# Two transformer layers on one core: FP4 input groups in two pieces, late key rounding at the slot's end, constant products placed anew

## What is computed

```python
h = _layernorm(x) * (1 + ca) + sa
x = x + ga * attention(h)              # layer 0: RoPE; one position beyond the causal mask
h = _layernorm(x) * (1 + cb) + sb
x = x + gb * ffn(h)                    # layer 0: FP4; layer 1: mixture of 8 experts, top 2, and a shared one

def fp4_quant_dequant(x):              # blocks of 16 along the last dimension
    scale = max(abs(block)) / 6
    idx = searchsorted(_MID, abs(block / scale))
    return _GRID[idx] * sign * scale
h = silu(fp4_linear(x, w_gate)) * fp4_linear(x, w_up)      # 352 wide
out = fp4_linear(h, w_down)
```

## Time and profile before

| | us |
|---|---|
| three runs, median | 727.2 |
| lowest, highest | 727.04, 727.38 |
| the profiled execution | 725.66 |
| its span, first to last instruction | 723.9 |
| TensorE busy, share | 640.5, 88% |
| VectorE busy, share | 473.1, 65% |
| ScalarE busy, share | 341.8, 47% |
| GpSimd busy, share | 225.4, 31% |
| mean granted clock of TensorE, of full | 0.974 |

### The profile page before, as it was taken

One profiled execution on the slowest core, in us unless ns is written; L12 is line 12 of the kernel. 1 busy time (PEld: TensorE's weight loads), 2 busy tenths in 40 slices (PEclk: granted clock), 3 DMA queues, 4 the chain that ended last, 5 costly groups with the idle time before them and its releaser, 6 DMA issues.

```text
span 723.9 us, 10992 instructions
## 1 busy us (share of the span) xinstructions
PE 640.5 (88%) x3840; PEld 497.7 (69%) x3858; DVE 473.1 (65%) x1258; ACT 341.8 (47%) x705; POOL 225.4 (31%) x247
## 2 busy tenths in 40 slices
PE   5788899998878989988899998968889997899996
PEld 4356687877656778774668786846678885576774
DVE  5956499675767557726569776586744436766665
ACT  1133454565535464543445465443555552554553
POOL 3325545453544211004555445264410002000000
PEclk9979999999989999999999999998999999999999
DMA  8400000000000000000000000000000000001001
GB/s 261 117 1 1 1 2 1 1 2 0 1 1 1 0 1 1 1 1 1 1 0 2 0 1 1 1 1 1 1 1 1 2 2 0 1 15 30 15 24 34
DMA packets 12077, 9.64 MB, mean 13 GB/s; under 512 B 1708, under 2 KB 10744, under 8 KB 12024
## 3 DMA queue, kind: packets, MB, share of 16 engines
q1 hardware_dynamic: 12024, 8.94, 4.2%
HBM read 6.84 MB, written 2.10 MB: 12 GB/s over the span
## 4 chain that ended last, share of the span: by engine, by line
PE 65%; DVE 16%; ACT 8%; POOL 7%; issue 4%; DMA 1%; SPq 0%; POOLq 0%; ACTq 0%; DVEq 0%
PE ps L787 14%; PE ps L657 12%; PE ps L765 8%; PE ps L936 4%; PE ps L938 4%; PE ps L937 4%; PE ps L616 4%; PE ps L810 2%; PE ps L675 2%; PE ps L811 2%; PE ps L826 2%; ACT xn L1053 2%; DVE xn L1339 1%; PE ps L838 1%; DVE xn L1258 1%
## 5 line engine op out<-in xcount | busy, mean ns | idle before, releaser
L1113 ACT ACTIVATE probsT<-ps 128x512 f32<-128x512 f32 (+3 forms) x160 | 85.3, 533 | 172.1 <-PE ps L765 172.1
L787 PE MATMUL ps<-v_sb,probsT 128*128 128x129 f32 (+1 forms) x1148 | 157.1, 280 | 3.7 <-ACT probsT L1115 3.7
L787 PEld LDWEIGHTS ps<-v_sb,probsT 128*128 128x128 f32 (+1 forms) x1148 | 141.5, 191 | 10.7 <-ACT probsT L1115 5.6
L1376 DVE TENSOR_REDUCE row_max<-ps 128x1 f32<-128x512 f32 (+2 forms) x144 | 88.2, 620 | 61.3 <-PE ps L657 26.3
L765 PE MATMUL ps<-ident,probs 128*128 128x128 f32 (+1 forms) x574 | 92.6, 278 | 14.6 <-ACT hT L1043 7.8
L1087 ACT ACTIVATE probs<-ps,neg_max 128x512 f32<-128x512 f32 (+7 forms) x158 | 92.7, 617 | 15.8 <-DVE neg_max L1383 12.0
L765 PEld LDWEIGHTS ps<-ident,probs 128*128 128x128 f32 (+1 forms) x574 | 65.4, 139 | 45.6 <-issue 41.8
L515 POOL TENSOR_TENSOR hq<-ha,hp 128x352 f32<-128x352 f32 x32 | 29.9, 933 | 128.7 <-DVE hp L1419 128.7
L657 PE MATMUL ps<-k_high,q_high 128*128 128x512 f32 (+4 forms) x110 | 44.9, 408 | 2.3 <-ACT probs L1087 2.2
L1188 ACT ACTIVATE probs<-ps 128x512 f32<-128x512 f32 x40 | 24.0, 599 | 44.8 <-PE ps L938 44.8
L1391 DVE RECIPROCAL rsum<-ps 128x1 f32<-128x1 f32 x64 | 10.5, 165 | 50.3 <-PE ps L787 50.1
(11 more groups left out here) (243 smaller groups left out, 1376.7 us busy)
## 6 DMA issues: line engine op xcount, KB each, us to landing
out<-x_sb SPq DMA_DIRECT2D x8, 256.0 KB, 2.3
x_sb<-in_L_attn_x SPq DMA_DIRECT2D x2, 512.0 KB, 5.5
hT_all<-in_L_wmod SPq DMA_DIRECT2D x2, 384.0 KB
rope_cos<-table_cos SPq DMA_DIRECT2D x1, 768.0 KB, 6.8
rope_sin<-table_sin SPq DMA_DIRECT2D x1, 768.0 KB, 8.3
rope_cos<-table_cos SPq DMA_DIRECT2D x1, 256.0 KB, 3.6
rope_sin<-table_sin SPq DMA_DIRECT2D x1, 256.0 KB, 4.9
moe_raw<-in_L_ffn_expert_gate_w SPq DMA_DIRECT2D x1, 256.0 KB, 3.9
```

The lines of the kernel that those rows point to most:

```text
L787: mm = pe.matmul(bank(OUT_AT, 0, V_W), probsT[0:size, n % 4, k * P:(k + 1) * P], v_sb[0:size, j, :], start=(c == 0 and k == 0), stop=(c == ...
L1113: ins = act.activation(probsT[:, n % 4, 0:full], bank(TURN, 0, full), ACT.Copy)
L1376: ins = dve.tensor_reduce(dst, ps[:, start:start + width], AX.X, ALU.max, negate=single)
```

## The change

- The FP4 input group is rounded by GpSimd and turned by TensorE in two pieces: tile 0 (key fp4_first) at slot 6 + 4g, tiles 1 to 3 (fp4_rest) at slot 7 + 4g. gate_up waits for the first with its tile 0 and for the rest with its tile 1. ScalarE copies the two pieces apart.
- ScalarE's normalise_1 signals each tile, and modulate_1 is eight instructions of 128 columns instead of two of 512. VectorE still waits for all four tiles.
- From slot 4 on, round_rope (ScalarE) stands at the slot's end, and rope_low (GpSimd) behind hq_scaled. This concerns Q2 in slot 4, K3 in slot 5 and Q3 in slot 6.
- Constant products: none at slot 6; 2, 8, 10 and 5 before the turns of norm2 groups 0 to 3 (slots 13, 17, 21, 25), after the wait for the bank and before that for the input; 11 in batch 0 and 18 in batch 1 before the last norm3 group instead of 9, and 4 behind it; 10 in the mixture of experts before the wait for the totals.

The diff, cut to its core:

```diff
+FP4_PARTS = ((0, 1), (1, GROUP))
-WAITS_AT_HEAD = {FFN_LAG: 11, TILES + 1: 8, TILES + 5: 10}
+WAITED_FOR = {("norm2", 0): 2, ("norm2", 1): 8, ("norm2", 2): 10, ("norm2", 3): 5}
...
-    firsts = (("fp4_in", FFN_LAG), ("norm2", DOWN_LAG + GROUP + 1), ("norm3", TILES + GROUP + 2))
+    firsts = (("fp4_first", FFN_LAG), ("fp4_rest", FFN_LAG + 1), ("norm2", DOWN_LAG + GROUP + 1), ("norm3", TILES + GROUP + 2))
...
                 def modulate_1(g):
-                    h = xn[:, g, :].rearrange("p (t d) -> p t d", d=P)
-                    row = lambda k: mod_row_now[:, k, :].unsqueeze(1).to_broadcast([P, GROUP, P])
-                    pool.wait_ge(xn1_ready, b * GROUPS + g + 1)
-                    pool.tensor_tensor(h, h, row(1), ALU.mult).then_inc(h_step, 1)
-                    pool.wait_ge(h_step, b * 2 * GROUPS + 2 * g + 1)
-                    pool.tensor_tensor(h, h, row(0), ALU.add).then_inc(h_step, 1)
+                    tiles = [xn[:, g, t * P:(t + 1) * P] for t in range(GROUP)]
+                    first = b * TILES + g * GROUP
+                    def add_shift(t):
+                        pool.wait_ge(h_scaled, first + t + 1)
+                        pool.tensor_tensor(tiles[t], tiles[t], mod_row_now[:, 0, :], ALU.add).then_inc(h_shifted, 1)
+                    for t in range(GROUP):
+                        pool.wait_ge(xn1_ready, first + t + 1)
+                        pool.tensor_tensor(tiles[t], tiles[t], mod_row_now[:, 1, :], ALU.mult).then_inc(h_scaled, 1)
+                        if t:
+                            add_shift(t - 1)
+                    add_shift(GROUP - 1)
...
                 def xq_scaled(g):
-                        pool.wait_ge(turned, TURN_AT[b, "fp4_in", g - 1] + 1)
-                    pool.tensor_tensor(xq[:], qa[:], qp[:], ALU.add).then_inc(xq_step, 1)
...
+                        pool.wait_ge(turned, TURN_AT[b, "fp4_rest", g - 1] + 1)
+                    for part, (a, z) in enumerate(FP4_PARTS):
+                        cols, done = slice(a * P, z * P), b * 4 * GROUPS + 4 * g + 2 * part
+                        pool.tensor_tensor(xq[:, cols], qa[:, cols], qp[:, cols], ALU.add).then_inc(xq_step, 1)
+                        pool.wait_ge(xq_step, done + 1)
+                        pool.tensor_tensor(xq[:, cols], xq[:, cols], qp[:, cols], ALU.subtract).then_inc(xq_step, 1)
...
                 for s in range(SLOTS):
-                    if early_group(s, K0_SLOT + 1) is not None:
-                        rope_low(early_group(s, K0_SLOT + 1), 0)
-                    if early_group(s, Q0_SLOT + 1) is not None:
-                        rope_low(early_group(s, Q0_SLOT + 1), 1)
+                    if s < FP4_SLOT:
+                        rope_lows(s)
...
                         hq_scaled(s - FFN_LAG)
+                    if s >= FP4_SLOT:
+                        rope_lows(s)
...
                 def turn_group(key):
-                    if kind == "fp4_in":
-                        pe.wait_ge(xq_ready, b * GROUPS + g + 1)
+                    if kind in ("fp4_first", "fp4_rest"):
+                        part = int(kind == "fp4_rest")
+                        pe.wait_ge(xq_ready, 2 * (b * GROUPS + g) + part + 1)
                         bank_free(key)
-                        for t in range(GROUP):
+                        for t in range(*FP4_PARTS[part]):
...
+                    bank_free(key)
+                    keep_clock(TURN, WAITED_FOR.get(key, 0))
...
-                    bank_free(key)
                     turn_normed(g)
...
                 def gate_up(n):
-                    if t == 0:
-                        out_of_bank(("fp4_in", g))
+                    if t < 2:
+                        out_of_bank((("fp4_first", "fp4_rest")[t], g))
...
-                    if s in WAITS_AT_HEAD:
-                        keep_clock(3, WAITS_AT_HEAD[s])
...
-                keep_clock(GATE, 9)
+                keep_clock(GATE, 11 if b + 1 < BATCH else 18)
                 turn_group(("norm3", GROUPS - 1))
+                keep_clock(GATE, 4)
...
+            pe.wait_ge(unselT_ready, 1)
+            keep_clock(0, 10)
             pe.wait_ge(totals_ready, 1)
...
                 def copy_group(key):
-                    if kind == "fp4_in":
-                        act.activation(xqT[:], bank(TURN), ACT.Copy).then_inc(copied, 1)
+                    if kind in ("fp4_first", "fp4_rest"):
+                        a, z = FP4_PARTS[kind == "fp4_rest"]
+                        act.activation(xqT[:, a * P:z * P], bank(TURN, a * P, z * P), ACT.Copy).then_inc(copied, 1)
...
+                def normalise_1(g):
+                    act.wait_ge(shift_ready, b * 2 * GROUPS + g + 1)
                     for t in range(GROUP):
+                        normalise(0, t, g).then_inc(xn1_ready, 1)
...
-                    if early_group(s, K0_SLOT + 1) is not None:
-                        round_rope(early_group(s, K0_SLOT + 1), 0)
-                    if early_group(s, Q0_SLOT + 1) is not None:
-                        round_rope(early_group(s, Q0_SLOT + 1), 1)
+                    if s < FP4_SLOT:
+                        round_ropes(s)
                     put_projected(s)
...
                             normalise_1(group_at(s, NORM1_SLOT + 1))
+                    if s >= FP4_SLOT:
+                        round_ropes(s)
...
-                    dve.wait_ge(h_step, b * 2 * GROUPS + 2 * g + 2)
+                    dve.wait_ge(h_shifted, b * TILES + (g + 1) * GROUP)
```

41 lines of the change are left out of this document (23 added, 18 removed).

## The result

The changed kernel takes 718.49 us (median of 4 runs, 717.74 to 719.83) against 727.29 us of the kernel before beside it: ratio 0.9887, 95% interval 0.9866 to 0.9908. The forecast was 717.8 us. The execution profiled took 719.19 us with a span of 717.4; that of the kernel before took 725.66 with 723.9. In later sessions the kernel before took 722.7 to 723.8 us in 11 of 40 executions and 725.4 to 728.3 in the others, so it scatters by more than the 727.04 to 728.47 us measured here; even so its lowest time lies above the changed kernel's highest.

The account below looks back on a forecast made before the run. TensorE, with 65% of the chain, was taken as the bound, so time is won where it waits or runs at the lower clock. Slots 6.6 us over two batches + 1.5 + 1.3 = 9.4 us; 727.2 - 9.4 = 717.8 us, range 712.5 to 724.0.

Parts of the forecast that it names:

- Price of a small GpSimd instruction: GpSimd: 128 columns cost 0.46 us (bounds 0.2 and 0.93), from 2.11 ns a column and 190 ns fixed.
- Rival (d): GpSimd's small instructions are dear, chiefly in modulate_1, so the kernel gets slower: 737.6 us at 1.0 us each; chance 0.04.
- modulate_1: GpSimd: eight 128-column instructions take 4.2 us against 2.6 in two, start 1.15 us earlier, end 0.35 us later.
- VectorE beside it: Slots 8, 12, 16: VectorE's wait for a started GpSimd instruction falls to at most 0.46 us; 0.3 us counted at slot 10.
- that rule alone: Shared-port lock: more GpSimd instructions mean more turns, FP4 rounding may come no earlier, losing 0.3 us per batch.
- Slot 6: Scores wait about 1.3 us for exp(6,0), gate_up under 0.5 for the copy; gains 1.5 us less 0.33 in slot 7.
- rival (a): The clock falls at slot 6 without its constant products, costing 1.4 us a batch: 720.6 us; chance 0.25.
- Slot 18: gate_up(12) 3.2 us earlier, 1.1 lost to one 3.4 us low-clock stretch: net 2.1 us a batch, less 0.33 in slot 19.
- rival (b): Slot 18's 1.2 GHz stretch stays (720.0), or products don't hold the clock at batch 0's end (719.3); both 721.5; chance 0.15.
- Slots 10 and 14: Slot 10 gains 1.0 us (0.7 to 1.2), slot 11 loses 0.33, slots 14 and 15 together lose 0.3, per batch.
- Constant products: In waits they cost nothing; the clock gives 1.5 us at batch 0's end, 1.3 at batch 1's slot 25, zero before mixture of experts.

Follow-up runs that it names:

- e1: Changed kernel with modulate_1 back in two 512-column GpSimd instructions after all four tiles: 720.11 us, ratio 0.9918.
- e7: Changed kernel with constant products added in slot 18's two waits, 3 before the first FP4 tile's turn and 12 before gate_up(12): 712.23 us.
- e2: Changed kernel with the rounding of the late rotated keys and their low parts back at the slot's head: 723.83 us, ratio 0.9969.
- e11: e8 with the rounding of the late rotated keys back at the slot's head: 716.56 us, ratio 0.9869.
- e6: Changed kernel without the two VectorE instructions forming the rounded step of silu tile 11 in slot 17: 711.43 us, ratio 0.9813.
- e3: Changed kernel with the FP4 input rounded and turned in one piece of four tiles: 718.35 us, ratio 0.991.
- e4: Changed kernel with the constant products where the kernel before had them: 719.05 us, ratio 0.9905.
- e12: e8 with the constant products where the kernel before had them: 717.26 us, ratio 0.9859.
- e8: Changed kernel with VectorE's rounding of silu tile 11, and GpSimd's scaling of it, moved from slot 17 behind q_low in slot 18: 708.67 us.
- e5: Changed kernel with 5 more constant products ahead of scores(7,0) in slot 6 of each batch: 717.7 us, ratio 0.9897.
- e9: e8 with FP4 input group 2 of each batch in one piece again: 707.68 us, ratio 0.9749.
- e10: e8 with every FP4 input group in one piece again: 719.16 us, ratio 0.9908.

## Why the prediction was right, point by point

**The bound and the total.** 717.8 was forecast and 718.49 measured. The steps of the forecast give 9.4 us; the profile's steps at the same places give 1.29 + 0.95 - 0.47 + 2.30 in batch 0, 1.29 + 0.95 - 0.47 + 0.72 in batch 1, 1.44 and 1.31: 9.3 us. What I had not foreseen (setup -1.84, slot 2 of batch 1 +4.52) adds up to +2.7 in the profile. So the near hit of the total has luck in it. These two stretches were in no term, and they happened to cancel in part; and batch 0's slots 16 to 19 gave more than forecast where batch 1's gave less than half.

**Price of a small GpSimd instruction.** Forecast 0.46 us for 128 columns by the slope of 352 and 512. Measured 0.456 and 0.460 for the FP4 sums, 0.504 and 0.468 for modulate_1, 0.403 for the last product: right. Rival (d) was out.

**modulate_1.** Forecast 4.2 us at 0.53 each, 0.35 us later than in two. It took 3.36 us, one every 0.41: products and sums of different tiles follow each other closer than the dependent chain of the first FP4 piece, which does keep 0.53 (194.86, 195.39, 195.92). VectorE starts earlier, not later; e1 puts 0.44 us to it in slot 5. The pessimism cost the forecast little.

**VectorE beside it.** This is the term that I had too small: I allowed 0.3 us at slot 10 and nothing elsewhere. By e1 the short instructions gave 0.54 us in slots 8 to 11 and, read against e7, 0.78 in slots 16 to 19 of each batch. They are also why the wait on xq in slot 18 was 0.76 us and not the 1.5 forecast: in e1 it is 1.56. The Trainium skill (SBUF — State Buffer, section "Who interferes with whom") has the shared port pair as an exclusive lock for the whole instruction; e1's 1.53 us against 0.81 agrees. I had added that by that rule alone the FP4 rounding could come out no earlier with more instructions, and it came out 0.8 us earlier. VectorE does meet GpSimd more often: from the product on, its three instructions take 0.81, 0.48 and 0.48 us in the changed kernel where e1 has 1.53, 1.30 and 0.34, and the scales' step at 191.60 takes 0.88 against 0.27. But each meeting is shorter: 1.4 us are won in the three and 0.6 lost in the fourth.

**Slot 6.** Forecast: scores wait for exp(6,0) (some 1.3 us), gate_up under 0.5 us, 1.17 us net. Measured: 1.22, 0.34, 1.29. Right, and no fall of the clock there: rival (a) did not come in the changed kernel. e2 and e11 show that the clock does fall there, in both batches, behind a wait of 2.7 us.

**Slot 18.** Forecast: wait on xq 1.5 us, then 2 to 3 on q_low, one low stretch of 3.4 us. Measured: 0.76, 2.93, low clock from 203 to 206 us in batch 0 and from 486 to 493 in batch 1. That VectorE's queue takes over was right, and e6 shows it. The sum was 3.2 us for the earlier gate_up(12), less 1.1 for the clock and 0.33 for slot 19. Counted from slot 15's reciprocal gate_up(12) came 3.8 us earlier (at 20.85 instead of 24.68), and the clock took 1.3 in batch 0 and 2.7 in batch 1 by e7. So batch 0 gave 2.3 us where 1.77 was forecast, and batch 1 only 0.72, as its low stretch was 6.8 us long like the one before and not 3.4: there the first half of rival (b) came true. Wrong was also whose merit the gain is. With the split undone (e3) the stage is 0.35 and 0.10 us longer, with modulate_1 undone 0.78: what ends last is VectorE's queue, and the short modulate_1 shortens that queue while the split doesn't.

**Slots 10 and 14.** -0.95 against -0.67, +0.47 against +0.3: small errors. In slot 10 the wait of 0.4 us for exp that I expected didn't appear, and VectorE gained more (0.54 by e1); in slot 15 the probabilities' turn also waits 0.32 us for the copy of the three tiles. TensorE, slots 10 and 15:

```profile
113.93 0.33 PE L725 MATMUL ps<-ident,xq 128*128 128x128 f32 x1
114.02 0.49 PE L675 MATMUL ps<-k_high,q_high 128*128 128x512 f32 x1
...
172.87 0.63 PE L785 MATMUL ps<-ident,probs 128*128 128x128 f32 x4 [0.32 <-ACT xqT L1056]
```

**Constant products.** The sizes hold: -1.44 at batch 0's end (1.5), -1.31 in slot 25 (1.3), nothing in the mixture of experts. Its turns start at 606.15 instead of 612.66 us, 6.5 us earlier, and all of that was won ahead of it. The products fill the wait for the totals (3.27 us before), and the two stretches of 3.4 us at 1.2 GHz that the kernel before had there are gone, without any gain in time:

```profile
606.15 1.96 PE L928 MATMUL ps<-ident_b,xn 128*128 128x128 bf16 x32 [2.06 <-DVE xn L1573]
...
609.19 2.33 PE L629 MATMUL ps<-unpick,ident_b 128*128 128x512 bf16 x9 [1.08 <-ACT v_sb L1203]
```

The cause doesn't hold as I gave it. In e4 both stretches are gone with the products in their old places. In e12 the one at batch 0's end is back. Which wait draws a low stretch depends on more than the work next to it. That products in waits help is shown by e7 for slot 18 (1.25 and 2.67 us, with nothing else moved). The medians say 6.3 us for e7 against the changed kernel and 8.6 for e12 against e8, but for the whole kernel, not for a place, and one run of e12 lost only 2.9.

**What stays open.** Why slot 2 of batch 1 ran at 1.2 GHz in the changed kernel, e1, e3 and e5 and not in the others, with the same instructions there; the setup likewise. No run changed only that. No kernel without any constant products was run, so what they are worth against none is not known. Nor was a second buffer for tile 12's scales tried, which would remove the wait at 205.75 in e8.

## What to carry to other kernels

Two waits one behind the other on the same engine hide each other: undoing one part of a change at a time (e3: 0.1 us) can call a part worthless that is worth 10 us once the other wait is gone. Look for what is late next, and remove that in the same step. And price an idle piece of TensorE with the clock that it may cost behind it, over the whole kernel and several runs, not at one place of one profile: with slot 18's wait filled or gone the runs of e7, e8, e9 and e11 lie within 0.4 to 1.5 us, but those of e12, where it is gone too, within 5.9; with the wait there, or some of it (the changed kernel, e1 to e6, e10), they lie within 2.1 to 7.6. So the wait is not all that scatters.
